# Causal mask of a two-layer attention kernel: added on TensorE before the exponential, or multiplied on VectorE behind it

## The reference

```python
def _L0_attn_ref(x, Wqkv_w, Wqkv_b, out_w, out_b):     # x: [8, 2048, 2048]
    qkv = jnp.einsum('bsd,ed->bse', x, Wqkv_w) + Wqkv_b
    q, k, v = 16 heads of 128 columns, one k and one v shared by all heads
    scores = jnp.einsum('bqhd,bkd->bhqk', q, k) * scale
    scores = jnp.where(causal[None, None], scores, min_val)
    ctx = softmax(scores) @ v
    return ctx @ out_w.T + out_b
x = _layernorm(x + _L0_attn_ref(x, ...))
# second layer: q, k, v of 16 heads each from x @ (Wa * col_scale), 8 tail columns
# per head taken from the low columns, the same causal softmax attention, then @ Wp
x = _layernorm(x + _L0_ffn_ref(x, Wa, Wp, w_std, w_rec))
```

## Time and profile before

| | us |
|---|---|
| runs shown (two) | 3859.24 and 3973.97 |
| median of the runs | 3916.61 |
| the profiled execution's own time | 3812.2 |
| its span, slowest core | 3810.6 |
| spans of the eight cores | 3764.9 to 3810.6 |
| TensorE busy in the span | 2913.8 (11150 matmuls) |
| ScalarE busy | 1098.4 |
| VectorE busy | 834.7 |

### The profile page before, as it was taken

The page is one execution under the profiler, slowest core; times in us unless marked ns, Lnnn a source line. Parts: engine busy times, 40 slices in busy tenths (PEclk is TensorE's granted clock), DMA queues, the critical chain, the costliest instruction groups (busy, mean ns, idle before and its releaser), DMA issues.

```text
span 3810.6 us, 32620 instructions; the slowest of 8 cores (3764.9 to 3810.6 us)
## 1 busy us (share of the span) xinstructions
PE 2913.8 (76%) x11150; PEld 1019.6 (27%) x11150; DVE 834.7 (22%) x1167; ACT 1098.4 (29%) x1922; POOL 108.3 (3%) x172
## 2 busy tenths in 40 slices
PE   1577763877787788991889877898777877788698
PEld 0222220222222222440334332333222222222243
DVE  0000001333333332332000000000333333333243
ACT  0011112444444453320111111112444444454121
POOL 1000000000000000000000000001000000000100
PEclk8788876887887889995999889789888878888799
DMA  9533348000000004997877668795200000000664
GB/s 142 102 67 65 66 88 139 16 21 21 21 16 21 21 16 88 255 210 142 147 163 184 158 137 156 161 190 156 50 20 21 21 16 21 21 21 12 151 194 144
DMA packets 516079, 348.71 MB, mean 92 GB/s; under 512 B 347728, under 2 KB 497232, under 8 KB 507728
## 3 DMA queue, kind: packets, MB, share of 16 engines
q10 hardware_dynamic: 174336, 167.78, 15.4%
q1 hardware_dynamic: 248672, 119.05, 13.4%
q0 software_dynamic: 92912, 59.79, 12.5%
HBM read 287.33 MB, written 75.50 MB: 95 GB/s over the span
## 4 chain that ended last, share of the span: by engine, by line
PE 63%; DMA 20%; DVE 5%; ACT 5%; issue 5%; SPq 1%; POOL 1%; DVEq 0%; ACTq 0%; POOLq 0%
PE proj_ps L827 10%; DMA vtok<-vstage 8%; PE proj_ps L295 8%; PE c1op_ps L593 6%; PE c2op_ps L593 6%; PE a2l_ps L510 5%; PE a2c_ps L513 5%; PE a1l_ps L510 5%; PE a1c_ps L513 5%; PE a2s_ps L489 2%; DMA x2t_win<-x2t_spill 2%; PE a2bc_ps L394 2%; PE a1s_ps L489 2%; PE a1bc_ps L394 2%; DMA wqT<-wqrows 2%
## 5 line engine op out<-in xcount | busy, mean ns | idle before, releaser
L827 PE MATMUL proj_ps<-x2t_win,wagrp 128*128 128x512 bf16 x3072 | 727.0, 402 | 194.5 <-issue 90.2
L498 ACT ACTIVATE a1ptile<-a1s_ps,a1mbias 128x512 bf16<-128x512 f32 (+3 forms) x640 | 392.0, 623 | 369.4 <-PE a1s_ps L486 186.6
L498 ACT ACTIVATE a2ptile<-a2s_ps,a2mbias 128x512 bf16<-128x512 f32 (+3 forms) x640 | 391.9, 623 | 318.1 <-PE a2s_ps L489 182.7
L827 PEld LDWEIGHTS proj_ps<-x2t_win,wagrp 128*128 128x128 bf16 x3072 | 312.3, 102 | 609.3 <-issue 339.5
L510 PE MATMUL a1l_ps<-a1ptile,ones_c 128*1 128x512 bf16 (+3 forms) x640 | 238.2, 372 | 123.4 <-DVE a1ctx_sb L399 54.4
L295 PE MATMUL proj_ps<-xT,wqT 128*128 128x512 bf16 x1152 | 307.2, 427 | 0.0
L510 PE MATMUL a2l_ps<-a2ptile,ones_c 128*1 128x512 bf16 (+3 forms) x640 | 237.9, 372 | 71.3 <-ACT a2ptile L498 50.2
L524 DVE RECIPROCAL a2recl<-a2l_ps 1x512 f32<-1x512 f32 x64 | 214.0, 3343 | 311.5 <-PE a2c_ps L513 305.2
L524 DVE RECIPROCAL a1recl<-a1l_ps 1x512 f32<-1x512 f32 x64 | 214.0, 3343 | 300.8 <-PE a1c_ps L513 300.8
L513 PE MATMUL a1c_ps<-a1ptile,vtok 128*128 128x512 bf16 (+3 forms) x640 | 247.6, 387 | 0.0
L513 PE MATMUL a2c_ps<-a2ptile,vtok 128*128 128x512 bf16 (+3 forms) x640 | 247.2, 386 | 0.0
(11 more groups left out here) (140 smaller groups left out, 1950.7 us busy)
## 6 DMA issues: line engine op xcount, KB each, us to landing
x2t_win<-x2t_spill ACTq DMA_DIRECT2D x48, 2048.0 KB, 10.2
qf_spill<-qstage SPq DMA_DIRECT2D x128, 128.0 KB, 1.8
c1x_win<-x ACTq DMA_DIRECT2D x16, 1024.0 KB, 11.8
x_spill<-c1y_rows SPq DMA_DIRECT2D x16, 1024.0 KB, 10.4
c2x_win<-x_spill ACTq DMA_DIRECT2D x16, 1024.0 KB, 10.7
out<-c2y_rows SPq DMA_DIRECT2D x16, 1024.0 KB, 9.0
wagrp<-wa POOLq DMA_DIRECT2D x32, 480.0 KB, 18.0
wqrows<-wqkv POOLq DMA_DIRECT2D x18, 512.0 KB, 5.3
```

What stands on the lines that cost most here:

```text
L498: s.activation(ptile[sb_i][:, 0:n], sp[:, (q0 - w * 512):(q0 - w * 512) + n], AF.Exp, bias=mbias[:, hb:hb + 1])),
L827: last = t.matmul(pst[:, :], wg[:, c * (GF * 128) + g_in * 128: c * (GF * 128) + (g_in + 1) * 128], x2t_win[wbx][:, c * SW2:(c + 1) * SW2] ...
```

## The change

In a diagonal step the mask is no longer added to the scores by a second matmul. The exponential is taken of the unmasked scores, and VectorE then multiplies the first 128 columns of `ptile`, in place, by a tile `mask01` of ones and zeros. `lpv` waits for that product where it waited for the exponential, since `tok_exp_bank` now holds VectorE's token; so does the score matmul that uses the same `s_ps` tile three steps later. GpSimd builds `mask01` in two instructions at the start. Nothing else is changed. A step that isn't diagonal is as before.

```diff
+    mask01 = sb0("mask01", [128, 128], BF16)
...
+    g_op(lambda g: g.memset(mask01[:, :], 1.0))
+    g_op(lambda g: g.affine_select(out=mask01[:, :], in_=mask01[:, :], compare_op=ALU.is_ge,
+                                   fill=0.0, base=0, pattern=[[1, 128]], channel_multiplier=-1))
...
                         def smm(t, sp=sp, c=c, w=w, q0=q0, q1=q1, h=h, hb=hb, n=n):
-                            if c >= 4 * w:
-                                j = c
-                                t.matmul(sp[:, (q0 - w * 512):(q1 - w * 512)],
-                                         kf_slice(h, c), qh[hb][:, q0:q1],
-                                         start=True, stop=False)
-                                return t.matmul(sp[:, (j * 128 - w * 512):(j * 128 - w * 512) + 128],
-                                                ident[:, :], maskT[:, :],
-                                                start=False, stop=True)
                             return t.matmul(sp[:, (q0 - w * 512):(q1 - w * 512)],
                                             kf_slice(h, c), qh[hb][:, q0:q1],
                                             start=True, stop=True)
...
+                        if c >= 4 * w:
+                            tok_exp_bank[sb_i] = P.do(
+                                "vector", (lambda v, sb_i=sb_i: v.tensor_mul(
+                                    ptile[sb_i][:, 0:128], ptile[sb_i][:, 0:128], mask01[:, :])),
+                                waits=[tok_exp_bank[sb_i]], inc="ve")
```

## The result

The changed kernel takes 4170.37 us (median of 11 runs, 4087.48 to 4230.78), the kernel before, measured beside it, 3886.33 us (10 runs, 3789.6 to 4006.15). The ratio is 1.0778, with a 95% interval from 1.0753 to 1.0803: slower by 7.8%. The forecast had slower by 3.4% and a range of 3925 to 4130 us. The direction was right; the loss is more than twice the size, and the median lies outside the range. In some executions, whatever the kernel, the four cores of one die show a lower clock than the others (six of these eleven; the other five took 4087 to 4103 us, inside the range); ratios leave these out, and where a kernel had nearly no others its shortest time is set against the shortest of before.

A forecast was written before the change was run, and what follows sets the result against it. The bound was taken as the loop exponential, lpv, score, exponential, not TensorE's busy time. Terms of 123, 1.9, 3.6 and 0.8 us made 130 us, 3.4%; the next median was put at 4020 us, range 3925 to 4130.

The forecast's parts named there:

- The mask matmul: Diagonal steps: it delays the exponential by 0.05 us; removing 512 gains 26 us if every one were on the path.
- The product: Between exponential and lpv in diagonal steps: 0.30 us a passage, 0.54 us for a third or fourth window.
- the product's own length: One VectorE product in a diagonal step: taken as 0.25 us, with ends of 0.22 and 0.29.
- The estimate from the Trainium skill: VectorE's product: two packed 16-bit elements a cycle, 224 ns; it would lower the sum by some 5 us.
- The queue behind the reciprocal: A head's first window: the first product waits on VectorE for the old window's reciprocal; spreading matmul 2.33 us later.
- the walk: First window, from reciprocal's end through product, lpv, score and exponential to the spreading matmul: at 42.25, not 39.92.
- the one on the clock: First window: TensorE's clock can fall before the lpvs; 0.4 us added, for 2.73 us in all.
- TensorE's 0.85 us: First window: TensorE's own part of the walk, about 0.85 us, which doubles at half clock.
- the third rival: Clock rises one window later, third window at half clock: 141 us more, 271 in all, 4083 us; chance 0.07.
- The ground given against it: Against the third rival: the clock rises from the second window's start, which the change leaves alone.
- The other ground: Against the third rival: TensorE is busy 18.19 of 20 us in a steady window.

The follow-up runs named there:

- the fill: Idle-work matmuls that nobody reads, here 14 of 512 columns while the first lpv waits for the reciprocal; in spread, products this gave 3863.52 us.
- third and fourth alone: Changed kernel with products only in the third and fourth window of a head, mask matmuls in the first two; 3860.41 us, ratio 1.0104.
- second to fourth, with fill: As products from the second on, plus a 256-column idle-work matmul ahead of each of the second window's last three lpvs; 3859.34, 4073.72 and 4083.97 us.
- both: Changed kernel with the mask matmul kept beside the product in every diagonal step; 4075.13 us, ratio 1.0647.
- spread, mask matmuls: Kernel before, with the next head's bias chain moved from behind the first window into four steps of the third; 3599.62 us beside 3815.12 before.
- neither: Changed kernel without the product, so no mask of either kind inside the diagonal blocks; 3819.82 us, ratio 0.9992 to before.
- spread, products: Changed kernel, products in all windows, with the next head's bias chain spread over four steps of the third window; 3999.5 us, ratio 1.0415.
- products from the second on: Changed kernel with products only in the second to fourth window, mask matmuls in the first; 4001.57 us, ratio 1.0457.
- spread, products from the second on: As spread, mask matmuls, but with products in windows two to four and mask matmuls only in the first; 3763.32 us, ratio 0.9874.
- first alone: Changed kernel with products only in the first window of a head, mask matmuls in the other three; 3913.56 us, ratio 1.0243.
- spread, fill in the first: As spread, products, plus 14 idle-work matmuls of 512 columns while a head's first lpv waits for the reciprocal; 3863.52 us, ratio 1.0161.
- second alone: Changed kernel with products only in the second window of a head, mask matmuls in the other three; 3966.77 us, no ratio.
- spread, all fills: As spread, fill in the first, plus 256-column idle-work matmuls ahead of the last three lpvs of each other window; 3732.58 us, ratio 0.9793.

## Why the prediction was wrong

**What held.** The mask matmul has almost no worth on the path: the forecast put it at 0.05 us a step and 26 us in all at most; a window without any mask is 0.17 us shorter, so 0.04 a step, and the kernel's time is where it was. The product lies between exponential and lpv and costs a window with the clock up 0.37 to 0.49 us, forecast 0.54; the product's own length came out at 0.22, forecast 0.25. The estimate from the Trainium skill that the forecast weighed ("VectorE: DVE Perf Modes": the rate by the section on what auto-detection checks, the fp32 formula by the one on the TRN2 errata) was 224 ns: the trace agrees, with 218 and 219. The queue behind the reciprocal works as the walk said: 2.27 us measured with the clock up, 2.33 forecast.

**The step that failed** is the one on the clock, in two places. In the first window the term was mis-sized: I put half of TensorE's 0.85 us, 0.4. With the clock held up by the fill that window takes 8.54 us, and 10.23 without, so the clock costs 1.69. It is down for the whole walk, which brings the spreading 0.7 us later, and the spreading takes 2.07 us where most heads of before needed 1.09. I had read one head, the one of the earlier trace rows, whose spreading had already paid for a part of it (1.75 us); the median over the heads would have shown it. The first windows grew by 112 us together, and the forecast had 82. In the third window the clock's term was missing: the forecast had 0.54 us, the product's path alone, and the measured window has 5.23, since the clock is down through most of it. The third windows grew by 145 us together, where the forecast had 16. The second and fourth grew by 22 and 12, forecast 9 and 16. That is 291 us; the first heads and the stretch between the attentions take 24 off, and 268 is left, where 130 were forecast.

This case stood in the text as the third rival, at 271 us on the profile's own time, for which 268 were measured. That the two agree so closely is luck: the rival had 157 us for the third windows (16 and 141), where 145 were measured, 43 less than measured for the first and second, and nothing for the 22 that fell away between the attentions. It got a chance of 0.07. The ground given against it, that "the work from which the clock rises, the second window's start, is not changed", is where it went wrong. The clock of before doesn't rise at the window's start but in its diagonal steps or right at their end, and these are just what the change thins out. The rows that show it were in hand: the first diagonal lpvs of that window still take 1.48 us from one to the next, and my own text said that the narrow steps behind them run at the upper clock. The other ground, TensorE busy 18.19 of 20 us, was read at full clock and by busy time; in the second window's diagonal steps 4.74 of 5 us are busy now, and no rise follows.

Even so the rival named the wrong cause as well as the right one. It laid the late rise on TensorE "standing 2.4 us longer" at the head's start. With that wait alone the third window stays at 12.51; with only the later windows' products it is at 16.7.

**What each run settles.** Third windows of 16 us and more, of 240 in the profiled execution of each:

| kernel | long | kernel | long |
|---|---|---|---|
| before | 0 | third and fourth alone | 0 |
| changed | 221 | second to fourth, with fill | 20 |
| both | 142 | spread, mask matmuls | 0 |
| neither | 0 | spread, products | 236 |
| products from the second on | 231 | spread, products from the second on | 143 |
| first alone | 0 | spread, fill in the first | 226 |
| second alone | 71 | spread, all fills | 0 |

The missing mask matmuls alone are not the cause (neither), but beside products they would soften it (both). The first window's wait costs 4 us a head and no more. Products in the third and fourth window by themselves cost only their path. Products in the second window are needed for the late rise; alone they bring it in some heads, with the later windows' in nearly all, and a fill in the second window's steps undoes it in most. In the spread schedule the clock is down for some 7 us of a head with mask matmuls, for 36 with products, and for 10 with products and all fills.

**What stays open.** With products in the second window alone, one core has the short third window in one attention and the long one in the other. I did not find what sets it on a given core, nor how the later windows' products add to it. Pauses and missing work were not taken apart. In the last head of each attention of the changed kernel, where nothing stands still behind the first window, the third window is short on all eight cores though the second holds products; in the kernel with products from the second window on it is long in 15 of 16 such heads. Nor did I try a fill in the changed kernel as it stands.

## What to carry to other kernels

Where TensorE's clock goes up and down within a loop, find in the trace at which instruction it rises, and treat that stretch as part of any change that adds a wait there: here products that leave pauses of some 0.3 us in it cost 5 us further on. Read it in several heads: the one that I read was not the usual one. Work that TensorE does in its own slack, such as adding a mask by a matmul, may be free however much busy time it shows, while the same work moved to an idle engine adds two semaphore hops to the path and stands behind whatever that engine has in its list. Before moving work, look for the standstill that sets the clock's trouble going: taking the bias chain out of the way was worth more than either form of the mask.

## What the hardware showed that I had not expected

Adding matmuls that compute nothing made a kernel faster, by 134 us in one case (3993.14 to 3859.34, the shortest of each; the other two runs with fill were longer) and, with the fill behind the reciprocal, by 246 in another (3963.15 to 3716.86, shortest runs). At the lower level of the clock the second window's diagonal steps with TensorE busy for 4.74 of 5 us by the profile were followed by no rise, while the same steps of the kernel before, with mask matmuls and without waits and 5.00 of 5 us busy, were.
